# Recurrent cell of a fused graph network: loop turn of four steps, TensorE's loop with a hint on its back edge, input gates in four buffers

## The chip, the cores and the metric

The kernel runs on one core of a Trainium2 chip. The metric is the device time of one execution in microseconds (us). The figures before are three executions, and one more that was profiled.

## The reference, cut to what matters

Eight layers follow each other on 625 rows of 512 numbers. The change touches one of them, a recurrent cell (an LSTM) that walks over the 625 rows one by one, with four sets of weights, of which each step picks one by the state that it starts from:

```python
def step(carry, x_t):
    h, c = carry
    sel_in = jnp.concatenate([h, c, x_t], axis=-1)
    logits = sel_in @ W_sel.T + b_sel
    onehot = jax.nn.one_hot(jnp.argmax(logits, axis=-1), Sx, dtype=x_t.dtype)
    g_all = jnp.einsum('bi,sgi->bsg', x_t, W_ih) + jnp.einsum('bh,sgh->bsg', h, W_hh) + b_ih + b_hh
    g = jnp.einsum('bsg,bs->bg', g_all, onehot)
    h2, c2 = _lstm_activate(g, c)
    return ((h2, c2), h2)
```

`_lstm_activate` splits the gates in i, f, g, o and returns `c_new = sigmoid(f) * c + sigmoid(i) * tanh(g)` and `h_new = sigmoid(o) * tanh(c_new)`. The first row takes set 0 and no state, so 624 steps with a choice remain. Each needs the h and c of the step before, so no two of them can be done side by side.

## The kernel before, in words

The program is a sequence of stages. `stage_input_gates` works out what the 625 inputs contribute to the gates, for all four sets, and stores it in the DRAM tensor `xg`. `stage_lstm` then runs the recurrence. Each engine has a program of its own in it, a loop of `LOOPS = 312` turns with `UN = 2` steps written out per turn (L1276, L1277); the engines meet through semaphores alone. A step is this:

- SyncE (L1312 to L1317) fetches the input gates of one step, for all four sets, by two DMAs of 16 KB into one of `UN` buffers of `xgb`. It may fill a buffer when TensorE has counted up `xg_used` (L1471); at the start TensorE gives it `UN` buffers (L1418).
- TensorE forms the four logits in `ps_logits`: the inputs' part (L1425), then the part of c (L1429) and of h (L1433). Between them stand two and one large multiplications whose result nobody reads (L1416).
- VectorE finds the largest logit (L1354, L1357). Meanwhile TensorE multiplies h by a part of the weights of all four sets (L1440, 32 small multiplications).
- TensorE loads the index of the best set into a register (L1457) and branches (L1473 to L1482). The code of `recurrent(e)` stands there four times, once for each set; a step runs one of the four copies and jumps over the other three. A copy is 24 + 32 multiplications at L1440 and four at L1470, which add the input gates.
- ScalarE and VectorE copy the rows out of PSUM (L1385, L1360), and TensorE turns them into columns (L1487, 16 multiplications of four f32 columns).
- ScalarE takes tanh of the gates (L1369), VectorE forms c (L1335, L1337), ScalarE tanh of c (L1371), VectorE h (L1342 to L1346). GpSimd keeps h (L1407).

At the end of a turn each engine steps its loop register and branches back (for TensorE at L1421). An f32 multiplication is issued as two in the trace, an f16 one as one, and each of them has a weight load (LDWEIGHTS) of its own ahead of it.

Of the kernel before, what the change touches and what calls it, by code (L numbers as in the profile page):

```python
# [857 lines left out]
def layer_ode(nc, x, ident, ones, w1t_in, b1_in, w2t_in, b2_in, b2_row_in, w3_in, w3t_in, b3_in, b3_row_in, whh_in, whh):  # L858
# [5 lines left out]
    DT = 1.0 / STEPS  # L864
    UN = 4
    CHUNK = GATES // 2
    with ExitStack() as ctx:
# [89 lines left out]
        with nc.Block() as block:  # L957
            @block.tensor
            def _(pe):
                def quarters(ps, w, col, start, stop):  # L960

                    for j in range(4):
                        m = nc.tensor.matmul(ps[32 * j:32 * j + 32, 0:1], w[:, 32 * j:32 * j + 32], col, start=start, stop=stop, skip_group_check=True)  # L963
                    return m
# [10 lines left out]
                quarters(ps_a, b2_parts, ones16[:], True, False)  # L975
                with pe.Fori(0, STEPS // UN) as i:
                    for r in range(UN):
                        k = i * (4 * UN) + 4 * r
                        q = r % 2
                        for s in range(4):  # L980
# [4 lines left out]
                            if s < 3:  # L985
                                if s == 0:

                                    pe.wait_ge(S["zb"], i * UN + (r + 1))
                                quarters(ps_u, ident, (zf if s == 2 else zh)[:], True, False)
                            else:  # L990

                                quarters(ps_z, m0_parts, ones16[:], False, False)
                                pe.wait_ge(S["p"], i * UN + (r + 1))
                                quarters(ps_z, mt_sixth, psum_b[:], False, False)
# [274 lines left out]
def stage_lstm(nc, whh, xg, xsel, wsel, ident, gsel, hist):  # L1269
# [3 lines left out]

    UN = 2  # L1276
    LOOPS = (N - 1) // UN  # L1277
    AHEAD = 2
    FIRST = 3 * 128
# [1 line left out]
    with ExitStack() as ctx:  # L1281
# [26 lines left out]
        with nc.Block() as block:  # L1308
# [101 lines left out]
            def _(pe):  # L1410
# [3 lines left out]
                def busy(n):  # L1414
                    for _ in range(n):
                        nc.tensor.matmul(ps_busy[:, 0:BANK], busy_w[:], busy_x[:, 0:BANK], start=True, stop=True)  # L1416
# [1 line left out]
                pe.sem_inc(S["xg_used"], UN)  # L1418

                nc.tensor.matmul(psc[:, 0:16], ident[:], xg0[:], start=True, stop=True).then_inc(S["gates"], 1)  # L1420
                with pe.Fori(0, LOOPS) as i:  # L1421
                    for q in range(UN):
                        k = i * UN + (q + 1)

                        nc.tensor.matmul(psl[0:1, 0:8], ones[:], xsel[:, ds(k * 8, 8)], start=True, stop=False, skip_group_check=True)  # L1425
                        busy(BUSY["c"])
                        pe.wait_ge(S["c_ready"], k)
                        for c in range(KC):
                            nc.tensor.matmul(psl[0:1, 0:4], ccur[:, c:c + 1], wsel[:, KC + c, :], start=False, stop=False, skip_group_check=True)  # L1429
                        busy(BUSY["h"])  # L1430
                        pe.wait_ge(S["h_ready"], k)
                        for c in range(KC):
                            m = nc.tensor.matmul(psl[0:1, 0:4], hcur[:, c:c + 1], wsel[:, c, :], start=False, stop=(c == KC - 1), skip_group_check=True)  # L1433
                        m.then_inc(S["logits"], 1)

                        def products(e, part, c, out, lo, hi):

                            for j in range(4):
                                at = e * CELL_COLS + (part * KC + c) * GATES + j * D
                                m = nc.tensor.matmul(out[32 * j:32 * j + 4, :], hpair[:, c, 2 - 2 * part:6 - 2 * part], whh[:, at + lo:at + hi],  # L1440
                                                     start=(part == 0 and c == 0), stop=(part == 1 and c == KC - 1), skip_group_check=True)
                            return m

                        def first(e, part, c):

                            return products(e, part, c, psg[:, e * BANK:e * BANK + FIRST], 0, FIRST)

                        pe.wait_ge(S["hp_ready"], k)
                        for c in range(AHEAD):
                            for e in range(CELLS):  # L1450
                                first(e, 0, c)
                        pe.wait_ge(xg_in[q], i * 32 + 32)
                        pe.sem_inc(S["seen_pe"], 1)

                        pe.wait_ge(S["best"], k)
                        pe.sem_inc(S["seen_pe"], 1)
                        s = pe.value_load(idx[0:1, 0:1])  # L1457

                        def recurrent(e):
                            for part in range(2):  # L1460
                                for c in range(KC):
                                    if (part, c) >= (0, AHEAD):
                                        m = first(e, part, c)
                            m.then_inc(S["rows_first"], 1)
                            for part in range(2):
                                for c in range(KC):
                                    m = products(e, part, c, psb[:, 0:D - FIRST], FIRST, D)
                            m.then_inc(S["rows_last"], 1)
                            for j in range(4):
                                m = nc.tensor.matmul(psc[32 * j:32 * j + 32, 0:16], ident[:, 32 * j:32 * j + 32], xgb[:, q, :, e * 8:(e + 1) * 8], start=True, stop=False, skip_group_check=True)  # L1470
                            m.then_inc(S["xg_used"], 1)  # L1471

                        with pe.If(s < 2):  # L1473
                            with pe.If(s < 1):
                                recurrent(0)
                            with pe.Else():
                                recurrent(1)
                        with pe.Else():
                            with pe.If(s < 3):
                                recurrent(2)  # L1480
                            with pe.Else():
                                recurrent(3)  # L1482

                        def turn(c):

                            for j in range(4):
                                m = nc.tensor.matmul(psc[32 * j:32 * j + 32, c:16:4], gsb[:, c * 128 + 32 * j:c * 128 + 32 * j + 32], gsel[:], start=False, stop=(c == KC - 1), skip_group_check=True)  # L1487
                            return m

                        pe.wait_ge(S["evac_a"], k)  # L1490
                        turn(0)
                        turn(1)
                        turn(2)
                        pe.wait_ge(S["evac_v"], k)
                        turn(3).then_inc(S["gates"], 1)
# [24 lines left out]
def layer_lstm(nc, x, ident, whh, wih_in, bih_in, bhh_in, wsel_h_in, wsel_x_in, bsel_in, gsel_in, xg):  # L1520
    with ExitStack() as ctx:
        def sb(name, shape):
            return ctx.enter_context(nc.sbuf_tensor(name, shape, F32))
        wsel, bsel, gsel = sb("l_wsel", [128, 2 * KC, CELLS]), sb("l_bsel", [1, CELLS]), sb("l_gsel", [128, 4])
        hist = sb("l_hist", [128, N, KC])
        xt = hist[:].rearrange("p n c -> p (n c)").rearrange("p (c n) -> p c n", c=KC)
        with nc.sbuf_tensor("l_xn", [TN, NT, D], F32) as xn:
            stage_layernorm(nc, "l_ln", ident, x, xn, xt)
        stage_input_gates(nc, xt, wih_in, bih_in, bhh_in, xg)
        wselx = sb("l_wselx", [128, KC, CELLS])  # L1530
        xsel = sb("l_xsel", [128, N * 8])
        load_all(nc, "lsel", [(wsel[:], wsel_h_in), (wselx[:], wsel_x_in), (bsel[:], bsel_in), (gsel[:], gsel_in)])
        stage_input_logits(nc, xt, wselx, bsel, xsel)
        scaled = new_semaphore(nc, "l_wsel_scaled")
        with nc.Block() as block:
            @block.vector
            def _(v):

                nc.vector.tensor_scalar(wsel[:, 0:KC, :], wsel[:, 0:KC, :], 1.0 / 2048, None, ALU.mult).then_inc(scaled, 1)
                nc.vector.tensor_scalar(wsel[:, KC:, :], wsel[:, KC:, :], 0.5, None, ALU.mult).then_inc(scaled, 1)  # L1540
                v.wait_ge(scaled, 2)
        stage_lstm(nc, whh, xg, xsel, wsel, ident, gsel, hist)
        stage_hist_out(nc, hist, ident, x)
# [353 lines left out]
```

## Time and profile before

| | us |
|---|---|
| three executions | 8438.53, 8421.07, 8441.01 |
| their median | 8438.53 |
| the profiled execution | 8436.44 |
| its span in the trace | 8434.8 |
| of this the recurrence (first to last row of L1425, L1440) | 4473.9 to 7996 |

The share of TensorE's clock over the whole span is 0.962. The page of the profile gives TensorE busy for 89% of the span, its weight loads 50%, VectorE 30%, ScalarE 20%, GpSimd 8%. In the row of forty slices TensorE is at 8 or more tenths in all of the recurrence and its clock at full speed. In rows of the timeline the first number is the start in us from the start of the span, the second the time from the first start to the last end of the instructions that the row merges, xN their number, and in brackets stands the idle time of the engine before it and what ended it; "issue" means that the engine waited for nothing that the profile shows. PEldq is the sequencer of TensorE that takes instructions from memory and hands them on. The lines "q8 instruction" are packets by which program text is fetched.

### The profile page before, as it was taken

The numbers are of one execution on the slowest core, as the hardware profiler recorded it, in microseconds if no ns is written. First come the engines' busy times: TensorE is split into PE (matmuls) and PEld (weight loads), VectorE is DVE, ScalarE is ACT, GpSimd is POOL, SyncE is SP. The second block draws the span as 40 slices with busy tenths as digits, with TensorE's granted clock in tenths as the row PEclk, the third lists the DMA queues.
The fourth block names the chain that finished last, engine by engine and source line by source line (L and its number), as shares of the span: only waits on it lengthen the run. The fifth ranks groups of instructions, "written<-read, shape, count | busy, mean of one in ns | idle before, by whom it ended". The sixth has DMA issues, their size and how long they took to land. (4 is left out here: it accounts for less than half of the span.)

```text
span 8434.8 us, 487838 instructions
## 1 busy us (share of the span) xinstructions
PE 7465.9 (89%) x211432; PEld 4251.9 (50%) x211432; DVE 2526.9 (30%) x12694; ACT 1708.8 (20%) x7657; POOL 697.1 (8%) x1191
## 2 busy tenths in 40 slices
PE   9879989999999999999798888888888888888851
PEld 7533334444444444444494555555555555555520
DVE  4327653211111111111242222222222222222248
ACT  0023222333333333333001111111111111111111
POOL 0014439400000000000000000000000000000000
PEclk9889989999999999999799999999999999999975
DMA  1023321000000000000130111111111111111100
GB/s 40 0 53 91 85 65 50 20 0 0 0 0 0 0 0 0 0 0 0 58 125 11 6 6 6 6 6 6 6 6 6 6 6 6 6 6 6 15 15 6
DMA packets 739821, 152.50 MB, mean 18 GB/s; under 512 B 694067, under 2 KB 708981, under 8 KB 739756
## 3 DMA queue, kind: packets, MB, share of 16 engines
q1 hardware_dynamic: 695596, 85.27, 6.8%
q0 software_dynamic: 40704, 45.90, 2.0%
q10 hardware_dynamic: 3456, 20.48, 0.6%
q8 instruction: 38, 0.62, 0.0%
q14 instruction: 27, 0.22, 0.0%
HBM read 123.19 MB, written 28.16 MB: 18 GB/s over the span
## 5 line engine op out<-in xcount | busy, mean ns | idle before, releaser
L969 PE MATMUL ode_busy<-ode_busy_x,ode_busy_w 128*32 128x320 f16 (+2 forms) x40000 | 2344.6, 311 | 46.5 <-issue 39.7
L1440 PE MATMUL ps_rows<-whh,h_pair 128*4 128x384 f16 x34944 | 1656.6, 326 | 185.9 <-issue 185.9
L1440 PEld LDWEIGHTS ps_rows<-whh,h_pair 128*4 128x4 f16 x34944 | 851.9, 84 | 741.0 <-issue 433.7
L963 PEld LDWEIGHTS ode_psa<-ode_a,ode_w2t 128*32 128x32 f32 x19968 | 411.4, 108 | 733.5 <-ACT ode_a L1018 577.2
L1385 ACT COPY gate_rows<-ps_rows 128x384 f32<-128x384 f32 x624 | 298.3, 478 | 2315.2 <-PE ps_rows L1440 2315.2
L969 PEld LDWEIGHTS ode_busy<-ode_busy_x,ode_busy_w 128*32 128x32 f16 x40000 | 712.8, 95 | 60.3 <-issue 60.3
L1360 DVE COPY gate_rows<-ps_rows_last 128x128 f32<-128x128 f32 x624 | 182.1, 292 | 1615.1 <-PE ps_rows_last L1440 1615.1
L1416 PE MATMUL lstm_busy<-lstm_busy_x,lstm_busy_w 128*128 128x512 f16 x1872 | 622.6, 387 | 0.0
L1020 ACT ACTIVATE ode_b<-ode_psa 128x1 f32<-128x1 f32 x2496 | 427.6, 171 | 952.3 <-PE ode_psa L963 952.3
L963 PE MATMUL ode_psa<-ode_a,ode_w2t 128*32 128x1 f32 x19968 | 602.9, 180 | 0.5 <-issue 0.5
L1018 ACT ACTIVATE ode_a<-ode_psu 128x1 f32<-128x1 f32 x1872 | 320.3, 171 | 725.8 <-PE ode_psu L963 725.8
L963 PE MATMUL ode_psa<-ode_ones,ode_b_parts 128*32 128x1 bf16 x9988 | 458.1, 163 | 0.0
L1407 POOL COPY l_hist<-h_now 128x4 f32 x624 | 116.2, 186 | 3406.8 <-DVE h_now L1342 3406.8
L1033 DVE SCALAR_TENSOR_TENSOR ode_part<-ode_b 128x1 f32<-128x1 f32 x624 | 114.7, 184 | 935.1 <-ACT ode_b L1020 935.1
L1440 PE MATMUL ps_rows_last<-whh,h_pair 128*4 128x128 f16 x19968 | 387.0, 219 | 0.0
L706 PE MATMUL msg_acc<-msg_m,msg_hot 125*125 125x512 f32 x724 | 373.6, 640 | 14.4 <-DVE msg_m L773 14.4
L1487 PE MATMUL ps_gates<-l_gsel,gate_rows 128*32 128x4 f32 x19968 | 317.1, 178 | 62.1 <-issue 6.8
L1440 PEld LDWEIGHTS ps_rows_last<-whh,h_pair 128*4 128x4 f16 x19968 | 328.5, 85 | 83.3
L963 PEld LDWEIGHTS ode_psu<-ode_b,ode_mt_half 128*32 128x32 f32 x9984 | 224.6, 108 | 244.0 <-ACT ode_b L1020 209.6
L1487 PEld LDWEIGHTS ps_gates<-l_gsel,gate_rows 128*32 128x32 f32 x19968 | 262.3, 110 | 123.2 <-ACT gate_rows L1385 116.2
L963 PE MATMUL ode_psu<-ode_zh,ident 128*32 128x1 f32 x9984 | 287.9, 174 | 24.9 <-DVE ode_zf L1031 17.6
L1429 PEld LDWEIGHTS ps_logits<-l_wsel,gates_and_c 128*1 128x1 f32 x4992 | 147.3, 81 | 312.2 <-DVE gates_and_c L1337 312.2
(432 smaller groups left out, 9065.2 us busy)
## 6 DMA issues: line engine op xcount, KB each, us to landing
xg_buf<-xg_scratch SPq DMA_DIRECT2D x1248, 16.0 KB, 1.9
split_raw<-in_whh_t SPq DMA_DIRECT2D x32, 512.0 KB, 3.5
ig_w<-in_wih_t SPq DMA_DIRECT2D x8, 2048.0 KB, 11.5
xg_scratch<-ig_out ACTq DMA_DIRECT2D x16, 832.0 KB, 3.7
xg_scratch<-ig_out ACTq DMA_DIRECT2D x8, 836.0 KB, 3.5
msg_h<-h_scratch SPq DMA_DIRECT2D x88, 62.5 KB, 2.7
h_scratch<-mlp_h SPq DMA_DIRECT2D x40, 125.0 KB, 2.3
msg_snd<-up_scratch,msg_idx POOLq DMA_INDIRECT x176, 5.5
```

The source lines that it names most:

```text
L706: mm = nc.tensor.matmul(acc[b][0:TN, :], hot[a % 2][:], m[a % 2][:, b * BANK:(b + 1) * BANK], start=False, stop=True, skip_group_check=True)
L963: m = nc.tensor.matmul(ps[32 * j:32 * j + 32, 0:1], w[:, 32 * j:32 * j + 32], col, start=start, stop=stop, skip_group_check=True)
L969: nc.tensor.matmul(ps_busy[32 * j:32 * j + 32, 0:cols], busy_w[:, 32 * j:32 * j + 32], busy_x[:, 0:cols], start=True, stop=True, skip_grou ...
L1018: nc.scalar.activation(a_col[:], ps_u[:, 0:1], ACT.Tanh).then_inc(S["a"], 1)
L1020: nc.scalar.activation(b_col[q][:, s:s + 1], ps_a[:, 0:1], ACT.Tanh).then_inc(S["b"], 1)
L1360: nc.vector.tensor_copy(gsb[:, FIRST:D], psb[:, 0:D - FIRST]).then_inc(S["evac_v"], 1)
L1385: nc.scalar.copy(gsb[:, 0:FIRST], psg[:, e * BANK:e * BANK + FIRST]).then_inc(S["evac_a"], 1)
L1407: nc.gpsimd.tensor_copy(hist[:, ds(k, 1), :], hcur[:]).then_inc(S["kept"], 1)
L1416: nc.tensor.matmul(ps_busy[:, 0:BANK], busy_w[:], busy_x[:, 0:BANK], start=True, stop=True)
L1429: nc.tensor.matmul(psl[0:1, 0:4], ccur[:, c:c + 1], wsel[:, KC + c, :], start=False, stop=False, skip_group_check=True)
L1440: m = nc.tensor.matmul(out[32 * j:32 * j + 4, :], hpair[:, c, 2 - 2 * part:6 - 2 * part], whh[:, at + lo:at + hi], start=(part == 0 and c ...
L1487: m = nc.tensor.matmul(psc[32 * j:32 * j + 32, c:16:4], gsb[:, c * 128 + 32 * j:c * 128 + 32 * j + 32], gsel[:], start=False, stop=(c == K ...
```

## The change

`UN` is 4 instead of 2. With it the loops of all five engines take 156 turns of four steps, `xgb` has four buffers, and SyncE may fetch up to four steps ahead. TensorE's loop alone is opened by another call, with `hint_back_edge=True`, which places one more instruction at the head of each turn that names the closing branch.

```diff
-    UN = 2
+    UN = 4
     LOOPS = (N - 1) // UN
...
                 pe.sem_inc(S["xg_used"], UN)
 
                 nc.tensor.matmul(psc[:, 0:16], ident[:], xg0[:], start=True, stop=True).then_inc(S["gates"], 1)
-                with pe.Fori(0, LOOPS) as i:
+                with nc.Fori(0, LOOPS, engines=[pe.engine], hint_back_edge=True) as i:
                     for q in range(UN):
                         k = i * UN + (q + 1)
```

TensorE's program at the head of the loop, before the change (`ps_logits` holds the four logits, `ps_rows` the products, `lstm_busy` the multiplications that nobody reads):

```order
L1420 MATMUL ps_gates<-xg_first,ident 128x16
L1421 UNCONDITIONAL_BRANCH
L1421 ISA
L1425 MATMUL ps_logits<-l_xsel,lstm_ones 1x8
L1416 MATMUL lstm_busy<-lstm_busy_x,lstm_busy_w 128x512 x2
```

The same place after it:

```order
L1420 MATMUL ps_gates<-xg_first,ident 128x16
L1421 UNCONDITIONAL_BRANCH
L1421 BRANCH_PREFETCH_HINT
L1421 ISA
L1425 MATMUL ps_logits<-l_xsel,lstm_ones 1x8
```

One instruction is new there, at the head of each turn. Below it, where the first turn's second step ended, the text of two more steps is put in on TensorE. This is a piece of it as it was added, from the load of the index to the end of the copy for the first set:

```order
+L1457 TENSOR_LOAD best_at
+L1473 COMPARE_AND_BRANCH
+L1474 COMPARE_AND_BRANCH
+L1440 MATMUL ps_rows<-whh,h_pair 4x384 x24
+L1440 MATMUL ps_rows_last<-whh,h_pair 4x128 x32
+L1470 MATMUL ps_gates<-xg_buf,ident 32x16 x4
+L1474 UNCONDITIONAL_BRANCH
```

The three other copies follow in the same form; the order inside a step is that of before, and only the number of steps between two back edges differs. On SyncE the turn grows from four DMAs to eight (L1317 writes `xg_buf`, the input gates of one step, in two halves):

```order
 L1317 DMA xg_buf<-xg_scratch 128x4x8
+L1315 REGISTER_ALU
+L1317 ISA
+L1317 DMA xg_buf<-xg_scratch 128x4x8
+L1317 ISA
+L1317 DMA xg_buf<-xg_scratch 128x4x8
```

The number of DMAs over the whole stage does not change.

## Rows read from the trace of the kernel before

**Rows 1.** Windows: busy time and count of each engine in the recurrence.

```profile
core 0: us, PE busy (x) PEld busy (x) DVE busy (x) ACT busy (x) POOL busy (x), PEclk, DMA share, GB/s
5000.00:6000.00 1000.00, 898.91 (x26494) 557.53 (x26490) 269.24 (x1777) 154.17 (x534) 33.16 (x178) 1.00 0.10 6
```

**Rows 2.** Timeline, TensorE, one turn of two steps.

```profile
6003.47 0.51 PE L1487 MATMUL ps_gates<-l_gsel,gate_rows 128*32 128x4 f32 x32
6004.25 0.19 PE L1425 MATMUL ps_logits<-l_xsel,lstm_ones 128*1 x2 [0.28 <-issue]
...
6009.22 0.51 PE L1487 MATMUL ps_gates<-l_gsel,gate_rows 128*32 128x4 f32 x32
6009.61 0.19 PE L1425 MATMUL ps_logits<-l_xsel,lstm_ones 128*1 x2
...
6014.72 0.51 PE L1487 MATMUL ps_gates<-l_gsel,gate_rows 128*32 128x4 f32 x32
```

**Rows 3.** Waits, 4500 to 8000 us, and TensorE's sequencer at the loop's own line.

```profile
PE ps_logits L1425 <- issue: 87.9, 310, 0.3
...
L1421 PEldq FUSED_REGOPS  x312: 78/78/88, 4473.5 to 7985.8; - x156
L1421 PEldq ALU_OP  x312: 36/36/39, 4495.2 to 7996.7; - x156
L1421 PEldq COMPARE_BRANCH  x312: 76/208/225, 4495.3 to 7996.8; - x156
```

**Rows 4.** The tile xg_buf: its DMA issues (ns min/median/max), and their landing.

```profile
L1317 SPq DMA_DIRECT2D xg_buf<-xg_scratch x1248: 372/373/1586, 4473.5 to 7985.8; - x179
...
DMA to landing us min/median/max: 1.8/1.9/3.3
```

**Rows 5.** Straight code at L1223, 4183 to 4430.5 us: TensorE's count, and its text packets.

```profile
4183.00:4430.50 247.50, 247.50 (x1407) 247.50 (x1406) 1.00 0.34 127
...
q8 instruction: 11, 0.18, 0.3%
```

**Rows 6.** DMA queues: the page (whole span), then 1240 to 1275, 1275 to 4000 us.

```profile
q8 instruction: 38, 0.62, 0.0%
...
q8 instruction: 7, 0.11, 1.3%
...
q1 hardware_dynamic: 3888, 14.16, 1.8%
```

**Rows 7.** DMA queues: 4473 to 4496, 4496 to 4574, 4574 to 4580, 4580 to 8000 us.

```profile
q8 instruction: 5, 0.08, 1.6%
...
q1 hardware_dynamic: 13728, 0.43, 9.6%
...
q8 instruction: 1, 0.02, 1.0%
...
q1 hardware_dynamic: 639936, 19.93, 10.2%
```

**Rows 8.** Timeline, TensorE, the first three steps of the loop.

```profile
4480.23 0.24 PE L1470 MATMUL ps_gates<-xg_buf,ident 128*32 128x16 f32 x8
4484.00 0.61 PE L1487 MATMUL ps_gates<-l_gsel,gate_rows 128*32 128x4 f32 x32 [3.52 <-issue]
4484.45 0.20 PE L1425 MATMUL ps_logits<-l_xsel,lstm_ones 128*1 x2
...
4491.60 0.29 PE L1487 MATMUL ps_gates<-l_gsel,gate_rows 128*32 128x4 f32 x10 [0.71 <-ACT gate_rows L1385]
4495.14 0.36 PE L1487 MATMUL ps_gates<-l_gsel,gate_rows 128*32 128x4 f32 x22 [3.25 <-issue]
4495.76 0.20 PE L1425 MATMUL ps_logits<-l_xsel,lstm_ones 128*1 x2 [0.25 <-issue]
```

**Rows 9.** Windows: the first two steps of the loop (columns as in rows 1).

```profile
4473.87:4484.45 10.58, 7.06 (x150) 4.17 (x150) 1.51 (x10) 0.87 (x3) 0.18 (x1) 0.66 0.18 12
4484.45:4495.76 11.31, 7.10 (x163) 4.14 (x158) 1.52 (x10) 1.05 (x4) 0.19 (x1) 0.78 0.07 7
```

## The prediction

> **What bounds the kernel now.** I read the windows first, to see where the time is: in the recurrence TensorE is busy for 899 of 1000 us at full clock, with 26494 multiplications in it [rows 1]. Then the timeline of one turn, for the length of a step: the turning multiplications of L1487 start at 6003.47, 6009.22 and 6014.72, so one step takes 5.75 us and the other 5.50, and a turn 11.25 [rows 2]. The stage is a chain of 624 dependent steps, so whatever delays a step on TensorE is paid in full. Third, what differs between the two steps: the 5.75 us one follows the back edge, and in it L1425 starts after 0.28 us of "issue", in the other after none [rows 2]; this happens 310 times in the waits [rows 3]. The sequencer shows what it does there, a branch of 208 ns in the median and a register step of 36 ns, together 0.24 us, and that is the 0.25 us between the steps [rows 3, 2]. Last I read the queues that fetch program text, because the change doubles the text of the turn and changes no operation of a step.
>
> **What goes: half of the back edges.** 156 fewer on TensorE, by 0.25 us: 39 us. The back edges of the other engines are halved too, but L1425 waits for "issue" on TensorE alone, and the others' lie under TensorE's work: 0. The waits that each step has stay as they are, with the same number of multiplications.
>
> **What is added in a turn: one hint instruction.** No row shows one. The nearest rows are TensorE's register instruction at the same line, 78 ns, and the branch, 208 ns [rows 3]; hidden behind queued multiplications it would cost 0. So 0 to 0.21 us by 156 turns, 0 to 32 us; I take the nearer 0.078, 12 us.
>
> **Four buffers for the input gates.** The DMAs land after 1.9 us in the median and 3.3 at most [rows 4]; with two buffers they are already issued a whole step of 5.5 us ahead, and no wait of TensorE for them stands in the trace. Fetching further ahead gives 0; the same 1248 DMAs are issued, and what is queued behind them on SyncE is only the next of them. If a burst of early loads at the start slowed the text packets, that would be once.
>
> **The text of the turn.** This is the term that decides. How much text is one packet? In straight code 11 packets of q8 come while TensorE runs 1407 multiplications and 1406 weight loads [rows 5], so 256 instructions per packet, and q8 is TensorE's. How long is a turn's text? A step has 1 + 2 + 4 + 1 + 4 + 32 multiplications ahead of the branch, four copies of 60 and 16 at the end, 300 as written. Of these 41 are f32 (1 at L1425, 4 at L1429, 4 at L1433, 16 at L1470, 16 at L1487) and are issued twice: 341, with as many weight loads 682, and with some 17 of branches, loads and registers 699. Two steps are 1398 instructions, 5.5 packets; four are 2797, 10.9 packets, lying on 11 or 12 of them. Only 306 or so of each 699 run, but a packet is fetched whole, and the copies that are jumped over are shorter than two packets (390), so nearly every packet of the turn is touched.
>
> What does fetching cost? The first turn shows it, because there the text is new. In the first step TensorE stands for 3.52 us at L1487, behind the jump over the other copies, and in the second for 3.25 us in the middle of the same line after 10 of 32 [rows 8]. Those two steps took 10.58 and 11.31 us, 21.89 against 11.25 in a later turn [rows 9, 2]. Part of the excess of 10.64 is the two stalls (6.77); the other 3.9 us goes with the granted clock, a mean of 0.66 and 0.78 in those steps [rows 9], that is parts at the 1.2 GHz level, where it is 1.00 later [rows 1]. Five packets came in these 23 us, one in the next 84, and none from 4580 to 8000 us, where only data queues stand [rows 7]. So before the change the loop's text is fetched once and kept. The middle-of-line stall shows something more: fetching runs at most one packet ahead of where TensorE is, since that next packet was still missing when a late jump into its neighbour reached the seam.
>
> Is a text of 10.9 packets kept as well? The trace bears on it from one side. The longest texts that it shows kept are this loop, 5.5, and the loop of the layer before, whose first turn brings 7 packets and which then runs to 4000 us without one [rows 6]. Over the span 38 packets came, 0.62 MB [rows 6], so nothing was fetched twice and nothing shows where the store ends. After the change the turn is 1.6 times the 7 packets that are the most seen kept. Bounds: all is kept, cost 0; or nothing is there when the turn comes round, and each turn pays as a first turn does. The upper one is 2 × 10.64 = 21.3 us per turn of four, by 156 is 3320 us.
>
> I count it a second way. If each packet is asked for only when its predecessor is entered, a turn can't be faster than 12 packets by 3.4 us (the mean of 3.52 and 3.25) = 40.8 us, against 22.5 now: 18.3 more. The hint can bring the first packet of the turn in early, which leaves 11 × 3.4 = 37.4, 14.9 more. I take the middle, 16.6, and 1 us for matmuls at the low clock that stick out beside the packets (the slow matmuls mostly lie under a packet's wait here, unlike the 3.9 of the first turn). 17.6 by 156 = 2746 us. Between the ends 0 and 3320 I take this since the nearest row in kind is the first turn of this very loop.
>
> The Trainium skill, "Runtime: NRT & Kernel Launch", section "Instruction fetch mechanics", gives TensorE an instruction memory of 128 KiB, 2048 instructions, filled in blocks of 256. The trace agrees with the 256 [rows 5]; the 2048 no row here shows. By it 1398 fit and 2797 don't, and the sum would be the one I take. The same section says that the memory is only two such blocks and that a taken branch whose target lies outside them waits for a fetch. Against that stands the trace: 312 back edges over 5.5 packets' worth, none over 225 ns, and no packet [rows 3, 7]. By this rule the loop before would already pay on each turn, and the change would only save back edges; its time is that of the first rival below.
>
> **Sum.** Against the profiled execution's own 8436.4 (span 8434.8, 1.6 us around it, 2.1 below the median of 8438.5): −39 + 12 + 2746 = +2719, so 11,155 us.
>
> **The rivals.**
> *All is kept, or comes in time (the other side: not slower).* The store holds 12 packets, and the change does what a longer turn does elsewhere. For it: no packet in 3420 us, and the 38 packets show no second fetch. Against it: nothing larger than 7 packets is seen kept. It decides from the point where the packets after the first turns stop. −39 plus 0 to 32: 8397 to 8429, with my 12 us 8409.
> *Partly kept.* If a new packet takes the place of one that lies in a fixed relation to it and not of the oldest, the middle of the turn stays. With 8 of 12 fetched per turn: two thirds of 2746 is 1831, so 8436 − 27 + 1831 = 10,240. For it: nothing rules it out. Against: it needs a special rule of placement.
> *The hint and the waits of a step hide most.* Each step has 3.3 us between its start and its branch, in which a packet can come. If the stalls are then one of 3.4 us per turn and not five or six, 156 × 3.4 = 530 and with some clock 700: 9110. Against it: the two stalls of the first turn came within 12 us of each other [rows 8].
>
> **Chances.** Forecast 0.62, partly kept 0.16, mostly hidden 0.10, all kept 0.12. What a measurement of this kernel can tell from none is about 0.3%, 25 us. All kept gives 7 to 39 us less, somewhat more often beyond 25 than within: faster 0.07, same 0.05. Slower is the rest, 0.88. The likeliest one's own range is 10,600 to 12,000 (16.6 down to 14 per turn, up to the 21.3 of the first turn and a little over). The range takes in the partly kept case and one more stall per turn at the top: 3320 + 156 × 3.4 = 3850 gives 12,260; at the bottom half of 2746 gives 9,780. I take 9,800 to 12,250, and leave outside nearly all of the last two cases.
>
> **What would show it.** Right: q8 packets all through the recurrence, some 1700 to 1900 in all and 25 to 30 MB, where there were 38; rows of L1487, L1440 and L1425 with 1 to 3.5 us of "issue" before them, several in each turn; PEclk below 1.00 in the stage and TensorE's busy share down from 90% to near 55%; the step still 5.5 us where no packet is awaited; all other stages unchanged. The branch at L1421 should stay near 0.2 us if the hint works and show 3 us if it doesn't. Wrong: no packets after the first turns and steps of 5.50, 5.50, 5.50, 5.75 us, which is the first rival; packets for a part of the turn alone (some 1250) is the second; packets everywhere with hardly a stall is the third. A time under 9,800 means that the fetches run further ahead than the first turn shows.

## The result and the profile after

The changed kernel takes 11,897.1 us (median of four, 11,891.7 to 11,908.4) against 8438.1 before (8421.1 to 8441.0): 3459 us more, a ratio of 1.4107, 95% interval 1.4082 to 1.4131. The forecast was 11,155 us with a range of 9,800 to 12,250. The profiled execution took 11,908.35 us.

The page of the kernel after, its lines on the whole span: TensorE's busy share, its forty slices, its granted clock, and the queue that fetches its text.

```profile
span 11906.7 us, 485966 instructions
PE 8542.2 (72%) x211432; PEld 4728.9 (40%) x211432; DVE 2533.1 (21%) x12694; ACT 1709.7 (14%) x7657; POOL 697.2 (6%) x1191
PE   8799899999999896666666665656666666566552
PEclk9899999999999897777777777777777777777775
q8 instruction: 1905, 31.21, 1.1%
```

The number of multiplications is that of before to the last one (211432), and so is the bulk of the data moved. New are the 1905 text packets, where there were 38 [rows 6], and the long stretch at 6 tenths with the clock at 7. Windows over the three parts show that only the recurrence changed (columns as in [rows 1]):

```profile
0.00:4478.00 4478.00, 4163.61 (x118004) 2209.34 (x118004) 1321.70 (x5452) 1113.68 (x5683) 580.60 (x565) 0.96 0.09 28
4478.00:11470.00 6992.00, 4237.90 (x92977) 2440.07 (x92976) 944.78 (x6241) 542.09 (x1873) 116.23 (x624) 0.75 0.07 7
11470.00:11906.00 436.00, 140.69 (x454) 79.50 (x454) 266.58 (x1002) 53.88 (x101) 0.39 (x2) 0.64 0.04 15
```

and the same three windows of the kernel before:

```profile
0.00:4474.00 4474.00, 4162.34 (x118004) 2212.34 (x118005) 1314.77 (x5452) 1114.27 (x5684) 580.45 (x565) 0.96 0.09 28
4474.00:7997.00 3523.00, 3161.99 (x92976) 1959.47 (x92974) 945.26 (x6240) 540.49 (x1873) 116.23 (x624) 1.00 0.10 6
7997.00:8434.00 437.00, 141.56 (x454) 80.04 (x454) 266.87 (x1002) 54.02 (x102) 0.39 (x2) 0.65 0.04 15
```

The recurrence grew from 3523 to 6992 us, 3469 more. TensorE is busy 1076 us more with the same 92977 multiplications, and idle 2754 us where it was 361: 2393 more. VectorE, ScalarE and GpSimd do what they did. Nearly all of TensorE's idle time stands ahead of four lines, as "issue", which its waits show (us in total, times, longest):

```profile
PE ps_gates L1487 <- issue: 1594.3, 609, 3.6
PE ps_logits L1425 <- issue: 465.9, 155, 3.4
PE ps_logits L1433 <- issue: 210.0, 153, 1.8
PE ps_rows L1440 <- issue: 187.6, 190, 3.4
PE ps_rows_last L1440 <- issue: 185.7, 146, 2.1
```

Before, L1487 waited for issue twice in the whole stage, in the first turn [rows 8], and L1425 for 0.3 us at most [rows 3]. The 188 us ahead of `ps_rows` are no new sum: there the wait for the index of the best set cost 186 us before (the line is shown below), though in 0.3 us each and not in long pieces. The timeline of a later turn shows where the stalls stand; it is the first turn's picture [rows 8] over and over:

```profile
8011.79 0.43 PE L1487 MATMUL ps_gates<-l_gsel,gate_rows 128*32 128x4 f32 x32 [2.93 <-issue]
8015.52 0.20 PE L1425 MATMUL ps_logits<-l_xsel,lstm_ones 128*1 x2 [3.30 <-issue]
...
8023.04 0.45 PE L1440 MATMUL ps_rows_last<-whh,h_pair 128*4 128x128 f16 x19 [1.68 <-issue]
...
8027.07 0.61 PE L1487 MATMUL ps_gates<-l_gsel,gate_rows 128*32 128x4 f32 x32 [3.53 <-issue]
...
8034.68 0.29 PE L1487 MATMUL ps_gates<-l_gsel,gate_rows 128*32 128x4 f32 x10 [0.24 <-ACT gate_rows L1385]
8038.16 0.44 PE L1487 MATMUL ps_gates<-l_gsel,gate_rows 128*32 128x4 f32 x19 [3.19 <-issue]
...
8046.26 0.44 PE L1487 MATMUL ps_gates<-l_gsel,gate_rows 128*32 128x4 f32 x32 [1.22 <-issue]
```

Each step stands still once or twice behind a jump or in the middle of a line. The starts of L1369 give the lengths of the four steps of a turn as 14.8, 11.1, 7.8 and 11.1 us in the mean, 44.9 together, where two old turns took 22.5. The slow clock shows in the length of single multiplications. After:

```profile
L1440 PE MATMUL ps_rows<-whh,h_pair 128*4 128x384 f16 x34944 | 2421.9, 435 | 190.1 <-issue 187.6
L1416 PE MATMUL lstm_busy<-lstm_busy_x,lstm_busy_w 128*128 128x512 f16 x1872 | 907.1, 549 | 0.0
```

Before:

```profile
L1440 PE MATMUL ps_rows<-whh,h_pair 128*4 128x384 f16 x34944 | 1656.6, 326 | 185.9 <-issue 185.9
L1416 PE MATMUL lstm_busy<-lstm_busy_x,lstm_busy_w 128*128 128x512 f16 x1872 | 622.6, 387 | 0.0
```

326 became 435 ns and 387 became 549: together 1050 us, where TensorE's whole busy time grew by 1076. The busy times of the groups overlap a little (all groups together grew by about 1225), so 1050 isn't an exact share, but these two make up most of it. The granted clock is at its full level, 2.4 GHz, for about half of the stage and at 1.2 GHz for the rest (mean 0.75).

The back edge itself, TensorE's sequencer at L1421:

```profile
L1421 PEldq BRANCH_PREFETCH_HINT  x156: 36/41/55, 4477.6 to 11427.9; - x156
L1421 PEldq COMPARE_BRANCH  x156: 85/2936/3349, 4516.8 to 11469.2; - x156
```

A median of 2936 ns, where it was 208 [rows 3]: even the packet that the hint names is waited for.

### The profile page after: what moved, and what is told of

It reads as the page before. It is cut to its first block and busy times, and to the rows that moved or that the text cites. A ratio compares the mean times of both kernels' runs of the same rounds, so it can differ in the third digit from the quotient of the medians.

```text
span 11906.7 us, 485966 instructions
## 1 busy us (share of the span) xinstructions
PE 8542.2 (72%) x211432; PEld 4728.9 (40%) x211432; DVE 2533.1 (21%) x12694; ACT 1709.7 (14%) x7657; POOL 697.2 (6%) x1191
## 3 DMA queue, kind: packets, MB, share of 16 engines
q8 instruction: 1905, 31.21, 1.1%
## 5 line engine op out<-in xcount | busy, mean ns | idle before, releaser
L1440 PE MATMUL ps_rows<-whh,h_pair 128*4 128x384 f16 x34944 | 2421.9, 435 | 190.1 <-issue 187.6
L1440 PEld LDWEIGHTS ps_rows<-whh,h_pair 128*4 128x4 f16 x34944 | 1283.9, 105 | 970.5 <-issue 421.1
L1487 PE MATMUL ps_gates<-l_gsel,gate_rows 128*32 128x4 f32 x19968 | 355.8, 185 | 1677.9 <-issue 1594.3
L1487 PEld LDWEIGHTS ps_gates<-l_gsel,gate_rows 128*32 128x32 f32 x19968 | 287.7, 129 | 1751.7 <-issue 1653.6
L1416 PE MATMUL lstm_busy<-lstm_busy_x,lstm_busy_w 128*128 128x512 f16 x1872 | 907.1, 549 | 0.0
L1440 PE MATMUL ps_rows_last<-whh,h_pair 128*4 128x128 f16 x19968 | 468.5, 225 | 185.7 <-issue 185.7
L1335 DVE SCALAR_TENSOR_TENSOR input_and_forget_part<-gates_and_c 128x8 f32<-128x8 f32 x625 | 104.7, 167 | 2026.4 <-ACT gates_and_c L1369 2026.4
L1440 PEld LDWEIGHTS ps_rows_last<-whh,h_pair 128*4 128x4 f16 x19968 | 387.3, 87 | 363.1 <-issue 313.1
L1425 PE MATMUL ps_logits<-l_xsel,lstm_ones 128*1 x1248 | 121.8, 171 | 465.9 <-issue 465.9
L1369 ACT ACTIVATE gates_and_c<-ps_gates 128x16 f32<-128x16 f32 x625 | 114.7, 183 | 2282.4 <-PE ps_gates L1487 2279.7
L1433 PE MATMUL ps_logits<-l_wsel,h_now 128*1 128x4 f32 x4992 | 235.6, 166 | 210.0 <-issue 210.0
```

## The experiments

The theory after the result: TensorE's store of text holds 8 packets of 256 instructions and drops the oldest (whether by when it was fetched or by when it was last used makes no difference in a loop that runs through its text, and no run here tells), a packet is asked for when the one ahead of it is entered, and a turn that needs more than 8 is fetched whole each time. The rivals: only what does not fit is fetched again; the longer turn or the four buffers cost something by themselves; the hint disturbs the fetching. All ratios are against runs of the kernel before on the same chip.

| run | turn of TensorE | us | ratio, 95% interval |
|---|---|---|---|
| e1_un4_nohint | 4 steps, no hint | 12,245 | 1.4525 (1.4502 to 1.4547) |
| e2_un3_nohint | 3 steps, no hint | 12,249 | 1.4528 (1.4502 to 1.4554) |
| e4_un2_hint | 2 steps, hint | 8483.8 | 1.0064 (1.0049 to 1.0080) |
| e5_two_un2 | 2 steps, text of two sets | 8341.9 | 0.9889 (0.9873 to 0.9906) |
| e6_two_un4_hint | 4 steps, two sets, hint | 8326.1 | 0.9872 (0.9855 to 0.9888) |
| e7_two_un4_slot0 | 4 steps, two sets, placed | 8307.1 | 0.9848 (0.9832 to 0.9865) |
| e9_two_un4_nohint | 4 steps, two sets | 9885.1 | 1.1726 (1.1705 to 1.1746) |
| e8_un4_late_hint | 4 steps, hint in last step | 12,035 | 1.4275 (1.4252 to 1.4299) |
| e12_un4_hint_slot0 | 4 steps, hint, placed | 11,407 | 1.3507 (1.3485 to 1.3530) |
| e10_others4 | 2 steps, the others 4 | 8433.5 | 1.0002 (0.9992 to 1.0011) |
| e3_un2_rotated | 2 steps, turned round | 8382.7 | 0.9944 (0.9931 to 0.9957) |
| e11_others4_rotated | the same, the others 4 | 8400.3 | 0.9963 (0.9949 to 0.9976) |

### The change without its hint, and three steps

```diff
-    UN = 2
+    UN = 4        # e1; UN = 3 in e2
```

> The change without the hint instruction. Theory A (the hint at the head of the turn brings nothing, all twelve text packets are waited for each turn): 11,890 us within 0.4%, some 1900 q8 packets, the branch at L1421 near 3 us. Rival (the hint does hide part of the turn's first packet): slower than 11,897 by up to 156 x 3 = 470 us. Rival (the hint disturbs the fetching): clearly below 11,897.

> Turn of three steps (3 x 699 = 2097 instructions, 8.2 packets, lying on 9), three input buffers, no hint. Theory A (the store holds 8 packets and drops the oldest, so a text just over it is fetched whole each turn): about 208 x 9 = 1870 packets in the loop, 3.5 us for most of them, so near the time of the four-step turn: 11,300 to 12,100 us. Rival (only what doesn't fit is fetched again): 208 x 2 or 3 packets, 9,200 to 10,000 us. Rival (the store holds 9 or more and less than 11): 8,425 us, no packets after the first turns.

Measured: 12,245 us without the hint, 348 us above the change. Theory A of e1 said 11,890 and is wrong in that part; its rival, that the hint is worth something, holds. Three steps take 12,249 us, a little above what the theory gave and far from both of its rivals. The queue of TensorE's text, in e1 from 4600 to 11,600 us:

```profile
q8 instruction: 1932, 31.65, 2.1%
```

and in e2 in the same window:

```profile
q8 instruction: 1983, 32.49, 2.2%
```

By the mean lengths of their turns (47.1 and 35.3 us) these are 13 packets per turn of four and 10 per turn of three. The four-step text lies on 12 packets and the three-step text on 9, so it is the whole turn and one more. The change has 1792 packets from 4600 to 11,300 us, 12 per turn. So "only what doesn't fit" is out: 8.2 packets' worth of text cost as much as 10.9. The back edge of e1, where the hint is missing, at L1421:

```profile
L1421 PEldq COMPARE_BRANCH  x156: 79/4797/5031, 4496.5 to 11797.2; - x156
```

4.8 us against 2.9. Without the hint two packets are asked for at the end of a turn, the next in the text, which nobody needs, and then the loop's first, and in the trace they overlap (the second starts 0.6 us after the first in the median and then takes 2.0 us instead of 0.9 to 1.5); with the hint the first is gone.

### The hint alone, on a turn that is kept

```diff
-                with pe.Fori(0, LOOPS) as i:
+                with nc.Fori(0, LOOPS, engines=[pe.engine], hint_back_edge=True) as i:
```

> The kernel before with the hint instruction alone, on a turn of two steps that is kept. Theory: the hint costs its own 0.04 us per turn, partly hidden: 312 x 0.04 = 13 us at most, 8438 to 8451 us, no packets in the loop. Rival (a hint makes the sequencer fetch): some hundred q8 packets more and a time above 8500 us.

Measured: 8483.8 us, 49 us more than before and 38 packets as before. The rival is out, but the price was expected too low, 13 us at most: 49 us by 312 turns is 0.157 us per turn. The hint's own record is short:

```profile
L1421 PEldq BRANCH_PREFETCH_HINT  x312: 36/36/55, 4465.3 to 8027.9; - x156
L1421 PEldq COMPARE_BRANCH  x312: 85/221/237, 4486.7 to 8039.0; - x156
```

It stands at the one place where the sequencer is late anyway, ahead of L1425, so it and the gap around it are paid in full: L1425 starts after 0.38 to 0.44 us of issue in this trace, against 0.28 [rows 2].

### The same loop with less text

To keep the work and take the text away, the copies for two of the four sets are left out:

```diff
-                        with pe.If(s < 2):
-                            with pe.If(s < 1):
-                                recurrent(0)
-                            with pe.Else():
-                                recurrent(1)
-                        with pe.Else():
...
+                        with pe.If(s < 1):
+                            recurrent(0)
+                        with pe.Else():
+                            recurrent(1)
```

and the same for ScalarE's copies. A step that picks set 2 or 3 then runs the copy of set 1, with as many multiplications: what these four kernels compute is another recurrence, and they tell of time alone. e5 is this with turns of two steps; e6, e7 and e9 have turns of four, with the hint, with the loop placed on a packet's first slot (`head_slot={pe.engine: 0}`) and plain.

> The kernel before with the text of two of the four sets left out on TensorE and ScalarE: steps that choose set 2 or 3 run the copy of set 1. The control for the next two runs. Same multiplications per step, one branch fewer: 8438 us less 0 to 100 us (up to 0.15 us a step for the branch). No packets in the loop.

> The full change (four steps, hint, four buffers) with the text of two of the four sets left out, as in its control: 1744 instructions per turn, 6.8 packets' worth, but by its place in the text lying on 8, and the fetch-ahead wants a ninth. Theory A (length of text is all that hurt, store of 8, oldest dropped): if the ninth is fetched each turn, the whole turn is thrown out and refetched: 156 x 8 to 9 packets, about 10,300 to 11,000 us; if it is not, the control less 39 us. Rival (the longer turn or the four buffers cost something of their own): above the control, without packets.

> Four steps, four buffers, no hint, the text of two of the four sets left out, and the loop's first instruction placed on the first slot of a packet, so that 1744 instructions lie on 7 packets and the eighth is the fetch-ahead. Theory A: all is kept, no packets after the first turns, the control less 39 us (156 back edges by 0.25 us), to within 15 us. Rival (a turn of four steps or four buffers are slow by themselves): at or above the control.

> Four steps, four buffers, the text of two of the four sets left out, no hint and no placement: 1743 instructions that lie on 8 packets. Theory A (the store holds exactly 8 packets, and without a hint the fetch-ahead at the end of the turn brings a ninth that throws out the first, so that the whole turn has to be fetched again): some 156 x 9 packets, 10,000 to 11,500 us. Rival (the store holds 9 or more, or the last packet is left too soon for the fetch-ahead): no packets after the first turns and the time of the placed one, 8307 us, within 15 us.

Measured: the control 8341.9 us; placed turns of four 8307.1, 35 us less, where 39 were expected; with the hint 8326.1, 16 us less, which is 39 for the back edges less 156 × 0.157 = 24 for the hint. Neither the longer turn nor the four buffers cost anything that these runs could tell, and that rival is out. e9, the same text on the same 8 packets as e6 but for the hint, takes 9885 us. From 4600 to 9300 us its text queue is at work:

```profile
q8 instruction: 1324, 21.69, 2.1%
```

With turns of 32.0 us that is 9 packets per turn: the 8 of the turn and the next in the text. In e6 no text packet comes from 4600 to 7800 us; this is the only line with a queue in that window:

```profile
q1 hardware_dynamic: 615882, 19.19, 10.5%
```

The two kernels differ by one instruction per turn, and by 1559 us. It also fixes the size: 8 packets are kept (e6), 9 are not (e9). The branches at the back edge say the same. e9, e6 and e7, in this order:

```profile
L1415 PEldq COMPARE_BRANCH  x156: 76/4390/4918, 4489.8 to 9441.8; - x156
```

```profile
L1415 PEldq COMPARE_BRANCH  x156: 85/221/237, 4491.8 to 7892.1; - x156
```

```profile
L1415 PEldq COMPARE_BRANCH  x157: 76/208/319, 4477.0 to 7881.1; - x157
```

My expectation for e6 left both ways open; e9 shows that the fetch-ahead was the danger and that the hint takes it away. e9 pays less per packet (10.2 us more per turn than e7's 21.8, for 9 packets) than the change. Its jumps are shorter, over one copy and not three, which I take for the reason, without a run that isolates it: only the first of its four steps is long, 13.0 us, the others 6.9, 6.0 and 6.1.

### When the hinted packet is asked for

e8 moves the hint from the head of the turn into its last step (the loop around it is opened by hand for this, with the same step of the register and the same branch at its end):

```diff
+                        if q == UN - 1:
+                            at_hint.append(nc.engines[pe.engine].mark_branch_hint_location())
                         pe.wait_ge(xg_in[q], i * 32 + 32)
```

> The change with the hint moved from the head of the turn to the last step, just before the index is awaited there, some 600 instructions of text and 5 us ahead of the closing branch. Theory (a hint at the head names a packet that is still there, and it is dropped in the course of the turn; a hint near the end fetches it in time): the branch at L1421 falls from 3 us to about 0.2 us, 156 x 2 to 3 = 300 to 470 us less than 11,897. Rival (the hint does nothing on this chip, or the one fetch queue is the bound so that the packet only comes in another order): 11,897 within 0.5%.

> The change with TensorE's loop placed on the first slot of a packet: its 2800 instructions then lie on 11 packets and not 12, and the last packet holds some 240 instructions of the turn and not a short piece. Theory (the hint makes the packet that is asked for on entering the last one be the loop's first, in place of the useless next one): 11 packets per turn, and it is asked for early enough, so that the branch at L1421 falls from 2.9 us to 0.2 to 1 us; with one packet fewer 156 x (2 + 3) = 780 us less than 11,897, 10,900 to 11,400 us. Rival (the hint only takes away the useless fetch and the first packet still comes on demand of the branch): the branch stays near 3 us, 11 packets, 11,300 to 11,600 us.

Measured: e8 12,035 us, 210 below no hint but 138 above the hint at the head, and its branch at 3116 ns in the median:

```profile
L1432 PEldq COMPARE_BRANCH  x156: 85/3116/3401, 4500.2 to 11560.9; - x156
```

It has the same 1905 packets as the change. A hint near the end doesn't bring the packet in time either; the theory behind e8 is wrong, and its rival said 11,897 within 0.5%, which it missed too. e12 places the loop so that it lies on 11 packets: 11,407 us, as its rival had it, with 1634 packets from 4600 to 10,800 us, 11 per turn of 41.7 us, and the branch no better:

```profile
L1421 PEldq COMPARE_BRANCH  x157: 85/3064/3501, 4475.7 to 10985.3; - x157
```

One packet fewer per turn is worth 490 us, 3.1 us a turn. The hint does bring the packet forward, but by too little. The traces have the start of each text packet. In e1 the useless packet starts 0.44 us after the branch at L1421 does, and the loop's first, which the branch asks for, at 1.03 us in the median and in none of 155 turns under 0.94; in e2, also without a hint, the least is 0.94 too. In the change and in e12 the loop's first packet starts at 0.44 us in the median: in the place and at the time of the useless one, so it isn't asked for by the branch. That is 0.6 us gained, and the branch still stands for 2.9. In both placements the last packet is mostly entered by the jump over the other copies, 66 instructions ahead of the branch. In 18 of e12's turns it is entered earlier, inside the copy of set 2, and still the loop's first starts 0.39 us after the branch does, so at which instruction it is asked for stays open. No run has more text between that point and the branch.

### The other engines' loops, and the back edge in another place

e10 leaves TensorE with two steps and two buffers and gives the other engines turns of four. e3 turns TensorE's loop round, so that its back edge stands where the sequencer waits for the index anyway:

```diff
+                head(1)
+                with pe.Fori(0, LOOPS - 1) as i:
+                    for q in range(UN):
+                        tail(i * UN + (q + 1), q, i)
+                        head(i * UN + (q + 2))
```

`head(k)` is the step's text up to the 32 multiplications of L1440, `tail(k, q, i)` the rest from `pe.wait_ge(xg_in[q], ...)` on. The last two steps are written out behind the loop. e11 has both edits.

> TensorE's loop as before (two steps), the loops of SyncE, VectorE, ScalarE and GpSimd with four steps, two input buffers. Theory (the back edges of the other four engines lie under TensorE's work): 8435 us within 0.2%. Rival (they are on the path too): up to 156 x 0.1 = 16 us less or more.

> Turn of two steps as before, but TensorE's turn starts behind the 32 multiplications of L1440 instead of at L1425: the back edge stands where its sequencer waits for the index of the best set (0.54 to 0.62 us idle there), the first head and the last two steps are written out outside of the loop. Theory: the 0.25 us of a back edge are hidden 311 times: 8438 - 78 = 8360 us, 0.9% faster, all steps 5.50 us. Rival (the back edge is paid wherever it stands): 8438 us, no change.

> The turned-round loop of TensorE (two steps) with the other engines' loops at four steps and two input buffers. The turned-round kernel alone took 8383 us and its step behind a back edge is still 0.06 us longer. Theory (the rest is TensorE's own: register step and branch end just after the index is there): 8383 us within 0.2%. Rival (the rest is the other engines' back edges, which the index now waits for): 8373 us, half of 312 x 0.06 us less.

Measured: e10 no change, as the theory had it. e3 8382.7 us, 0.56% faster than before (interval 0.43% to 0.69%) and the fastest of all kernels here that do the whole work; 52 of the expected 78 us. Its timeline has no issue gap ahead of the line that forms the logits' first part, which is L1435 there (L1425 is the products' line there):

```profile
6002.40 0.51 PE L1487 MATMUL ps_gates<-l_gsel,gate_rows 128*32 128x4 f32 x32
6002.78 0.20 PE L1435 MATMUL ps_logits<-l_xsel,lstm_ones 128*1 x2
...
6006.23 1.15 PE L1425 MATMUL ps_rows<-whh,h_pair 128*4 128x384 f16 x24 [0.34 <-issue]
6007.96 0.51 PE L1487 MATMUL ps_gates<-l_gsel,gate_rows 128*32 128x4 f32 x32
6008.35 0.20 PE L1435 MATMUL ps_logits<-l_xsel,lstm_ones 128*1 x2
...
6011.73 0.50 PE L1425 MATMUL ps_rows<-whh,h_pair 128*4 128x384 f16 x8 [0.29 <-issue]
```

The branch still takes 208 ns, beneath the wait for the index, and what is left shows behind the load of it, 0.34 us of issue instead of 0.29. The steps are 5.57 and 5.51 us in the mean.

e11 was to tell whose the rest is, and with 8400 us it is no faster than e3. The two were measured on different chips and their intervals just touch, but the traces tell where e11 loses. The recurrence takes 13 us longer than in e3 (3478.2 against 3465.2 us), all of it in every fourth step, 5.66 us where the step that e3 has there takes 5.57. It is the step behind VectorE's back edge: there VectorE begins its search for the largest logit (L1354 before, L1357 in e11) 0.46 us after the last multiplication of the logits starts, in the others 0.32. Its next instruction starts 0.33 us after its branch does, in e3 0.20. So the longer loop has the slower back edge on VectorE, and once TensorE's own is out of the way it is on the path; why it is slower no run shows. The 0.06 us that are left in e3 are TensorE's own: behind its back edge it starts to load the index 0.25 us after VectorE's result, else 0.19.

## Why the prediction was right

**Direction and range.** Right, by the mechanism that the sum rested on: the text of the turn is no longer kept. The windows, the 12 packets per turn and e7 show it. One step of its reasoning was weaker than it looked: the jumped-over text of 390 instructions can hold a whole packet, so that "nearly every packet is touched" did not follow. All 12 are fetched all the same, as the next packet is asked for whether it will be run or not. e7 also bears out the small terms: with the text out of the way, turns of four on all engines with four buffers give 35 us, against the 39 of the back edges and the 0 of the buffers.

**The first rival, all kept.** Out by the 1792 packets. The point that it named as decisive, the packets after the first turns, decided.

**The second rival, partly kept.** Out: 12 of 12 packets per turn, and e2 with 10 of 9 + 1 for a text that is 0.2 packets over.

**The third rival, hidden in the waits.** Out in the main: the waits above are 1063 in 156 turns, leaving `ps_rows` aside, nearly seven per turn and not one. It is at work in part, for seven waits are fewer than twelve packets, and in the shortest of the four steps, 7.8 us in the mean, packets come while TensorE works.

**The hint.** Its own price was put at 0.078 us per turn out of bounds of 0 to 0.21; e4 has 0.157, between the bounds. Its benefit was put at half a packet's wait, 1.7 us per turn, by bringing the loop's first packet early. The benefit is 348 us by 156 turns, 2.2 us, but mainly by another way: it takes the useless thirteenth packet off. The first comes 0.6 us earlier and is still waited for. The sign that the prediction named, a branch at L1421 of 0.2 us if the hint works and 3 us if it doesn't, showed 2.9 us, while e1 has 4.8. That the size came out near is luck in this term.

**The size: 3459 us measured, 2719 forecast.** The term that was mis-sized is the one for the clock. The chain of packets was taken at 16.6 us of added standing per turn, with back edges and hint −39 and +12: 2563 us. Measured are 2393 us more idle time. (The two are not quite of a kind: the forecast's term is how much longer the turn gets by its packets, whatever TensorE does meanwhile.) For matmuls at the low clock that "stick out beside the packets" the forecast took 1 us per turn, 156 us, with the reason that they lie under a packet's wait. Measured are 1076 us more busy time, 6.9 us per turn, nearly all of it in L1440 and L1416, whose single multiplications take 435 for 326 and 549 for 387 ns. They don't lie under a wait. The stretch between two stalls of the timeline above shows it, columns as in [rows 1]:

```profile
8027.07:8034.68 7.61, 7.37 (x150) 4.33 (x150) 1.44 (x10) 0.87 (x3) 0.19 (x1) 0.58 0.01 4
```

A step's work without a wait for text takes 7.61 us at a mean clock of 0.58, where a step took 5.50. The next packet that this work runs into is asked for only once it gets there, so the 2.1 us come on top of that packet's wait. Per packet the turn takes 44.9 / 12 = 3.74 us, where the chain had 3.4, the two stalls of the first turn without the slow work between them. The other way of counting, the first turn's excess of 10.64 us per two steps [rows 9], held the clock in it and gave 3320, 4% below the 3459 measured. The choice to go below it was the error. That the clock and not something else stretches these multiplications is read from the granted clock beside them; no run isolated it, and none splits the 3459 us into text and clock except by this account.

**The size of the store.** The Trainium skill, "Runtime: NRT & Kernel Launch", section "Instruction fetch mechanics", says that TensorE's instruction memory holds 2048 instructions and is refilled in blocks of 256. The runs agree with it: 8 packets are kept and 9 are not (e6, e9). Its other rule, two blocks, is out for TensorE by the same runs. The same section of the Trainium skill calls the cost of crossing a block's boundary mostly hidden. In straight code the trace agrees, TensorE is busy for all of 247.5 us in which 11 packets come [rows 5]; behind a jump that came late into the block ahead, the crossing in the middle of L1487 costs 3.19 us.

## What to carry to other kernels

Before a loop is unrolled further, count the instructions of the turn, all copies of a branch with them, and compare with the longest text that the trace shows being kept; past the edge it isn't the excess that is paid but the whole turn, on each turn. A first turn in the trace is a measurement of what a turn costs when its text isn't there, clock included, and should be taken whole. And a back edge costs nothing where the sequencer waits for something anyway: moving it there got 52 us (interval 36 to 58), at least what halving their number got where the text was kept, 35 (e7 against e5).

## What the runs showed of the hardware

- In these runs TensorE keeps 8 packets of 256 instructions, 16 KB each (e6, e7). One above that and every packet of the turn is fetched on each turn (9 in e9, 10 in e2, 13 in e1).
- On entering a packet the next in the text is asked for, needed or not. At the end of a loop that fills the store this one useless packet costs the whole of it: 9885 against 8326 us (e9, e6). A hint that names the back edge prevents it, for 0.157 us a turn, and brings the loop's first packet 0.6 us forward (the change against e1).
- A packet that isn't there holds TensorE for up to 3.6 us, 2.6 in the mean at L1487, and in the stage behind such stalls about half of the time is at the 1.2 GHz level: 1076 us of longer multiplications came with 2393 us of standing still.
- One level of branch less per step, on TensorE and ScalarE, gave 93 us (e5 against before); by the turns, 11.00 and 11.25 us, 78 of them are in the recurrence, 0.125 us a step.
